# A kernel of two attentions with experts: who copies the first half of the turned probabilities in the late batches

## What is computed

```python
x = L0_attn_x
xn = _layernorm(x, axis=-1)
x = x + _L0_attn_ref(xn, ...) + _L0_ffn_ref(xn, ...)
xn = _layernorm(x, axis=-1)
x = x + _L1_attn_ref(xn, ...) + _L1_ffn_ref(xn, ...)
return x
```

```python
scores = jnp.einsum('bhid,bhjd->bhij', q, k) / scale
alibi = -distance[None, :, :] * _slopes(N_HEADS)[:, None, None]
scores = scores + alibi[None]
scores = jnp.where(causal[None, None], scores, -jnp.inf)
attn = jax.nn.softmax(scores, axis=-1)
out = jnp.einsum('bhij,bhjd->bhid', attn, v)
```

## Time and profile before

| | us |
|---|---|
| median of three runs | 2551.15 (2551.03 to 2551.17) |
| the profiled execution | 2551.31 |
| its span in the profile | 2549.6 |
| late batches in it, first reduction to last values | 1563.46 to 1673.5, 110.0 |
| start of the third stage's loads | 1678.27 |

### The profile page before, as it was taken

How to read it: one execution, slowest core, us unless ns; L and a number is a source line. 1 busy time by engine, 2 the same in 40 slices (tenths; PEclk the granted TensorE clock), 3 DMA queues, 4 the chain that set the end, 5 groups by cost and what they waited for, 6 DMA issues and landing times. The chain is left out here.

```text
span 2549.6 us, 90401 instructions
## 1 busy us (share of the span) xinstructions
PE 2301.5 (90%) x34944; PEld 1795.8 (70%) x34944; DVE 1737.0 (68%) x7187; ACT 1664.9 (65%) x5470; POOL 799.1 (31%) x879
## 2 busy tenths in 40 slices
PE   6999997889899899899899988779999799999998
PEld 5888886667777777777677776557777566666665
DVE  6777773567777777777777776612111389888888
ACT  2333332777777777777777777843433499999988
POOL 3666665021111111111111112300000456566562
PEclk9999998899999999999999999989999899999999
DMA  7866542666666666667667663023322111111110
GB/s 239 240 156 183 126 99 66 156 156 164 164 169 171 171 168 170 163 160 174 170 157 173 171 167 90 20 85 92 110 86 86 46 27 39 29 34 40 28 38 14
DMA packets 360914, 305.80 MB, mean 120 GB/s; under 512 B 25384, under 2 KB 328872, under 8 KB 358968
## 3 DMA queue, kind: packets, MB, share of 16 engines
q1 hardware_dynamic: 350008, 272.97, 42.7%
q0 software_dynamic: 10496, 27.28, 3.6%
HBM read 167.47 MB, written 132.69 MB: 118 GB/s over the span
## 5 line engine op out<-in xcount | busy, mean ns | idle before, releaser
L823 ACT ACTIVATE probs<-neg_scores,low 128x256 f32<-128x256 f32 (+1 forms) x1152 | 574.3, 500 | 247.3 <-DVE low L959 236.3
L959 DVE CUSTOM_DVE_ANT_0 neg_scores<-scores,rel_bias 128x256 f32<-128x256 f32 x1024 | 373.7, 421 | 256.1 <-PE scores L1122 113.5
L1136 PE MATMUL probsT<-consts,probs 128*128 128x128 f32 x2240 | 363.3, 285 | 56.6 <-ACT probsT_s L839 51.8
L1136 PEld LDWEIGHTS probsT<-consts,probs 128*128 128x128 f32 x2240 | 250.3, 143 | 113.3 <-ACT probsT_s L839 71.7
L774 POOL TENSOR_SCALAR q_heads<-q_raw,consts,q_bias 128x256 f32<-128x256 f32 x128 | 69.7, 559 | 756.9 <-ACT q_raw L805 756.8
L1579 DVE CUSTOM_DVE_ANT_0 neg_scores<-scores,alibi 128x128 f32<-128x128 f32 (+1 forms) x896 | 266.2, 353 | 56.6 <-PE scores L1635 53.3
L275 POOL TENSOR_TENSOR hid<-hid,gate_bc 128x512 f32<-128x512 f32 x160 | 205.5, 1289 | 151.2 <-DVE hid L448 139.7
L967 DVE COPY rel_s<-scores 128x768 f32<-128x768 f32 x256 | 244.0, 953 | 5.3 <-PE scores L1122 3.9
L301 ACT ACTIVATE ga<-gate_up 128x512 f32<-128x512 f32 x160 | 95.7, 598 | 223.2 <-PE gate_up L514 221.5
L1541 ACT ACTIVATE probs<-neg_scores,low 128x128 f32<-128x128 f32 (+1 forms) x448 | 199.7, 448 | 52.3 <-DVE low L1579 43.7
L1293 ACT ACTIVATE he<-up,b1e 128x512 f32<-128x512 f32 (+1 forms) x192 | 111.7, 617 | 183.0 <-PE up L1271 182.9
(11 more groups left out here) (194 smaller groups left out, 4873.5 us busy)
## 6 DMA issues: line engine op xcount, KB each, us to landing
rel_rows<-rel_s SPq DMA_DIRECT2D x256, 192.0 KB
rel_bias<-rel_rows SPq DMA_DIRECT2D x256, 192.0 KB, 3.5
gate_bc<-gate_rows SPq DMA_DIRECT2D x32, 1024.0 KB, 10.6
rel_rows<-rel_s SPq DMA_DIRECT2D x256, 128.0 KB
rel_bias<-rel_rows SPq DMA_DIRECT2D x256, 128.0 KB, 3.0
packed<-ffn_in SPq DMA_DIRECT2D x8, 1280.0 KB, 15.7
xe<-packed SPq DMA_DIRECT2D x16, 640.0 KB, 4.3
expert_out<-ye POOLq DMA_DIRECT2D x16, 640.0 KB, 6.9
```

The costliest lines, as they stand in the source:

```text
L823: act.activation(probs[s % 3][:, j, 0:w], neg[s % 2][:, j, 0:w], ACT.Exp, bias=low[s % 3][:, j:j + 1], scale=-1.0, accum_out=sums[s // UB ...
L959: dve.tensor_tensor_reduce(neg[s % 2][:, j, 0:w], S_ps[:, 512 * j:512 * j + w], bias_of(s)[:, j, :] if s < NU0 else alibi[:, 4 * j + s % 4 ...
L1136: ins = pe.transpose(PT_ps[:, j * P:(j + 1) * P], probs[u % 3][:, j, kt * P:(kt + 1) * P], ident)
```

## The change

For the units from 256 on, the first-half copy leaves ScalarE's list and comes into VectorE's, behind the four reductions of the step and ahead of its other work. It waits there for the same three things as before on ScalarE: the first turn, and that the values (and relative values) that used the place in `probsT` are done. The second-half copy of these units stays on ScalarE, and as it can no longer rely on ScalarE's own order, it gets the two waits for the place in `probsT`.

```diff
--- before.py
+++ after.py
@@ -831,17 +831,20 @@
                         if s % UB == 0 and s >= 2 * UB:
                             act.wait_ge(inverted, s // UB - 1)
                         exps(s, 0)
-                    if 0 <= u < NUL:
+                    if 0 <= u < NU0:
                         act.wait_ge(turned, halves_turned(u) + 1)
                         if u >= 8:
                             act.wait_ge(valued, u - 7)
-                            act.wait_ge(rel_valued, min(2 * nb, (u - 8) // 4 + 1))
+                            act.wait_ge(rel_valued, (u - 8) // 4 + 1)
                         act.copy(probsT[:, u % UB // 4, u % 4, 0, :, :].rearrange("p j q -> p (j q)"), PT_ps[:, :]).then_inc(moved0, 1)
                     if 0 <= s < NUL:
                         exps(s, 1)
                         exps(s, 2)
                     if 0 <= u < NUL and width(u) == S:
                         act.wait_ge(turned, halves_turned(u) + 2)
+                        if u >= NU0:
+                            act.wait_ge(valued, u - 7)
+                            act.wait_ge(rel_valued, min(2 * nb, (u - 8) // 4 + 1))
                         act.copy(probsT[:, u % UB // 4, u % 4, 1, :, :].rearrange("p j q -> p (j q)"), PT_ps[:, :]).then_inc(moved1, 1)
                     if 0 <= s < NUL:
                         exps(s, 3)
@@ -959,6 +962,12 @@
                             dve.tensor_tensor_reduce(neg[s % 2][:, j, 0:w], S_ps[:, 512 * j:512 * j + w],
                                                      bias_of(s)[:, j, :] if s < NU0 else alibi[:, 4 * j + s % 4, S - w:S],
                                                      1.0, 3e38, ALU.add, ALU.min, low[s % 3][:, j:j + 1]).then_inc(lowest, 1)
+                    u = s - 2
+                    if NU0 <= u < NUL:
+                        dve.wait_ge(turned, halves_turned(u) + 1)
+                        dve.wait_ge(valued, u - 7)
+                        dve.wait_ge(rel_valued, min(2 * nb, (u - 8) // 4 + 1))
+                        dve.tensor_copy(probsT[:, u % UB // 4, u % 4, 0, :, :].rearrange("p j q -> p (j q)"), PT_ps[:, :]).then_inc(moved0, 1)
                     u = s + LEAD - 1
                     if 0 <= u < NU0:
                         dve.wait_ge(scored, u + 1)
```

## The result

| | before | changed |
|---|---|---|
| median of 12 runs each | 2551.16 us | 2557.01 us |
| profiled execution (span) | 2551.31 (2549.6) | 2556.78 (2555.1) |
| late batches, first reduction to last copy of a context | 1563.46 to 1673.73, 110.27 | 1563.90 to 1679.61, 115.71 |
| start of the third stage's loads | 1678.27 | 1684.12 |

The ratio of the runs is 1.0033, 95% interval 1.0020 to 1.0045, so the changed kernel is slower. The medians are 5.85 us apart; the ratio, which is that of the means (2550.3 and 2558.7), stands for 8.4 us, its interval for 5.1 to 11.5. In the profiled pair the late batches are 5.44 us longer and the barrier 5.85 later; 0.44 of that was there before the first late unit. Behind the barrier nothing is lost: the whole execution differs by 5.47.

The account below looks back on a forecast made before the run. The prediction took a loop of waits through TensorE, ScalarE and VectorE, with no engine full, to bound the late batches. Its terms gave 2551.31 + 5.3 (steps) + 1.3 (clock) - 0.16 = 2557.7 us, 8-in-10 range 2552 to 2563.5.

Parts of the forecast that it names:

- the case forecast: Whole run: slower, 2556.5 to 2559.5 us, chance 0.53.
- What bounds the kernel: Late batches, units 256 to 287: TensorE, ScalarE and VectorE wait in turn in a loop; no engine is full.
- First term: Eight late steps: the copy lengthens VectorE's list, delaying the next reduction; +4.3 us.
- Second term: Late steps: VectorE copies only behind all four reductions, so the second turn comes later; +2.4 us.
- Third term: Steps 260 and 276: relieved ScalarE moves the keys earlier, so the v projection waits less; -1.4 us.
- Fourth term: Late batches: longer TensorE waits may bring one more stretch at half clock; 0 to 2.6 us, taken as 1.3.
- ScalarE's relief decides: Rival: late waits shrink as ScalarE's list loses 18.5 us; faster, down to 2532.7, or 2542 with half; chance 0.07.
- Hidden: Rival: the copy falls into VectorE's waiting for scores in light late steps; no change, 2552 to 2554 us; chance 0.25.
- The clock falls more often: Rival: longer TensorE pauses bring two or three more half-clock stretches, 2.6 us each; 2562 to 2564 us; chance 0.15.

Follow-up runs that it names:

- narrow kernel: Changed kernel, but only the copies of narrow late units (16 of 32) on VectorE, ScalarE keeping those of wide ones; ratio 0.9996.
- wide kernel: Changed kernel, but only the copies of wide late units on VectorE; ratio 1.0011.
- second pair: Kernel before and changed kernel, both run once more unchanged in the same visit; ratios 0.9997 and 1.0026, late batches 107.55 and 112.52 us.
- list experiment: Kernel before, with an unused 128x512 addition on VectorE at the copy's place in each late step, ScalarE keeping its copies; ratio 1.0001.
- two-copies kernel: Kernel before with only the first-half copies of units 257 and 273 on VectorE; ratio 0.9977.
- kernel before with filler: Kernel before, with six unused matmuls on TensorE ahead of the second turn in steps 270, 278 and 286; ratio 0.9991.

## Why the prediction was right, and where its terms were not

Forecast 2557.7, measured 2557.01, inside the range of 2552.0 to 2563.5; the case forecast is the one that came. That the two are only 0.7 us apart is luck: the 12 executions of the kernel before lie between 2544 and 2555, and the ratio's interval is 6 us wide. By its own steps:

*What bounds the kernel* held: a ring of waits, no full engine. ScalarE lost 15.65 us of busy time and the stretch grew.

For the size of the terms I take step differences at full clock, from either pair of profiles or from the narrow and wide kernels (for 278 3.48 - 3.01, for 279 3.37 - 2.94). The end, from the last unit's first reduction to the last context copy, is from the second pair (9.31 to 9.84).

| term | predicted | measured |
|---|---|---|
| first, VectorE's list: 264, 267, 269, 270, 275, 277, 280, 283 | +4.3 | +0.61, 0.61, 0.58, 0.31, 0.17, 0.94, 0.85, 0.28: +4.35 |
| second, later turn: 262, 263, 265, 271, 272, 273, 278, 281, 286 and the end | +2.4 | +0.47, 0.11, 0.18, 0.43, 0.03, 0.11, 0.47, 0.17, 0.07, 0.53: +2.57 |
| third, ScalarE's keys' move: 260, 276 | -1.4 | -0.70, -0.87: -1.57 |
| not in the sum: 261, 279, 268 | 0 | +0.12, +0.43, -0.05: +0.50 |
| sum | +5.3 | +5.85 |
| fourth, clock | +1.3 | 0 in two profiled pairs; on average open |

- *First term.* The sum is right because errors cancel. Step 277 was put down as list only, +0.61; its copy also waits for the turn, which stands behind the v projection in TensorE's list. Step 280 has the longer gap that the list experiment showed too. Steps 264, 275 and 283 lost less than predicted. Step 270 lost 0.31 in the first pair, and 0.58 in the second (3.02 to 3.60), where VectorE's list had no slack there in the kernel before either; with that value the sum would be 0.27 more.
- *Second term.* Its parts add up to 2.47, which the prediction rounds down to 2.4. The working "1.38 + 0.69 + 0.06 = 2.13" measured 2.11 in step 278. The experiment with ScalarE's copy made later shows that the place costs without VectorE's load, the one with an addition for nobody that the load costs without the place, each in the steps named for it as far as these could be read.
- *Third term.* Confirmed by leaving only it: the narrow kernel and the two-copies kernel have it, the wide one doesn't. Step 260 gave 0.70 where 0.56 was said.
- *Step 279*, left out, is the largest missing one: at half clock it was bound by the turn, in the stretch that begins in the earlier trace rows, so I saw no room for the copy to matter; at full clock it loses 0.43 like 271. A step read at half clock hides what bounds it at full clock.
- *Fourth term.* It did not come in the profiled pairs: TensorE's wait in 278 grew to 3.04 us as said, but the clock lost no more. The windows of 4 us give for the late batches a loss of 6.8 us of full clock before and 6.8 after, and 3.4 in both of the repeated pair. What it rested on, that a longer wait brings more half clock, is not borne out: waits of 2.4 to 2.6 us ahead of this turn left the clock full in three kernels. But two pairs can't say that the term is 0 on average. Of the ten executions of the repeated changed kernel the mean granted clock was 0.0014 lower than of the kernel before, which over 2545 us is an estimated 3.6 us of full clock, and the ratios stand for 6.7 and 8.4 us where the steps explain 5.85. So some clock loss beyond the steps may be there; no profile shows where. In the profiled pairs the stretches moved: to 1640 to 1648, 1652 to 1660 and 1664 to 1672 in the changed kernel, from 1636 to 1644 and 1660 to 1668. In the first pair they fell on steps that took some 0.4 us off the difference (5.85 to 5.44 measured).

With the clock at 0 and the terms as measured, the sum would be 2551.31 + 5.85 - 0.16 = 2557.0. Against the medians the prediction's 2557.7 had 0.5 too little in steps and 1.3 too much in clock, two errors that partly cancel. That the steps' 5.85 is also the difference of the medians is chance, as the means say 8.4.

The rivals. *ScalarE's relief decides*: no; 15.65 us less on it bought two steps, 1.57 us. By the Trainium skill (Perfetto Trace Analysis, Identifying the Most-Contended Engine) the engine of highest occupancy, here ScalarE at 82% of the stretch, is to be optimised first; this measurement goes against it. *Hidden*: in some steps it was so (258, 259, 266, 268, 274, 282, 284, 285 unchanged within 0.05), but most of the steps that got a copy grew. *The clock falls more often*: not in the changed kernel's two profiles; the wide kernel's profile had such a case (0.93 in place of 0.97 over its late batches), while its ratio was 1.0011.

## What to carry to other kernels

In a ring of waits an engine's load says little: ask in each step which list the next link waits for, and price a moved instruction there twice, by its length on the list that ends last and by its new place in time. Here half of the moved copies cost little (0.47 us), as they also freed a move of keys that others waited for, and the other half some 4 us or more; a move that helps should be made only for the units where it does. A shorter wait in every batch isn't yet a gain: look which wait takes its place, and repeat a gain of 0.2 to 0.4% on another chip before you believe it.

## What the runs showed beside

The two visits of 2765 us. Pauses of 4 to 8 us stand in a late step while GpSimd issues the indirect writes of the packed rows (line 793), and VectorE and, for a part of it, TensorE stand still. From the kernel before with filler:

```profile
1693.79 0.42 DVE L959 CUSTOM_DVE_ANT_0 neg_scores<-scores,alibi 128x256 f32<-128x256 f32 x1 [4.95 <-remote]
```

The profile calls what ended the wait remote. In these visits every second batch of the first attention, from the sixth on, takes some 40 to 42 us and the others 34 to 38; in the other visits all take 33 to 38. By the first late unit the kernels are some 70 to 100 of the 220 us behind. The cause isn't known; one issue lasts 0.96 us in either kind of visit.

The first stretch of the second stage varies by itself: from the first reduction to the first late one it took 1120.1 us in the first profile of the kernel before and 1108.9 in its repetition, a difference larger than the whole effect measured here, so differences that small must be read from the steps, or from medians of many runs.
